# Attention sums of a graph layer: taken out of PSUM by ScalarE and added by GpSimd instead of VectorE

## What is computed

```python
deg = clip(adj.sum(axis=1), 1.0); dis = deg ** (-0.5)
diffusion = (dis[:, None] * adj * dis[None, :]) @ x - x
sim = x @ x.T / (norms[:, None] * norms[None, :])
attn = softmax(beta * sim * adj, axis=1)
x = layernorm(x + diffusion + sigmoid(alpha) * (attn @ x - x))
x = layernorm(x + relu(adj @ (x @ weights)))
```

## Time and profile before

| | before |
|---|---|
| median of 3 runs | 679.48 us |
| profiled execution: its time, its span | 679.01 us, 677.2 us |
| TensorE (PE) busy, share of the span | 652.0 us, 96% |
| VectorE (DVE) busy | 561.9 us, 83% |
| ScalarE (ACT) busy | 436.2 us, 64% |
| GpSimd (POOL) busy | 245.5 us, 36% |
| mean granted TensorE clock | 0.996 |
| DVE instructions L724 and L727 | 32 each, about 0.34 us each |

### The profile page before, as it was taken

The page is one execution under the profiler, slowest core; times in us unless marked ns, Lnnn a source line. Parts: engine busy times, 40 slices in busy tenths (PEclk is TensorE's granted clock), DMA queues, the critical chain, the costliest instruction groups (busy, mean ns, idle before and its releaser), DMA issues.

```text
span 677.2 us, 17913 instructions
## 1 busy us (share of the span) xinstructions
PE 652.0 (96%) x5623; PEld 517.4 (76%) x5623; DVE 561.9 (83%) x1678; ACT 436.2 (64%) x885; POOL 245.5 (36%) x229
## 2 busy tenths in 40 slices
PE   6679999999999999999999999899999999999997
PEld 6347777777777777777777776799888888888886
DVE  4879999999999999999999999767767766666664
ACT  5989998998999999989999988512222223111111
POOL 2899446455455464454464557300000000000000
PEclk8999999999999999999999999999999999999999
DMA  6589999999999999999999994300000000000000
GB/s 252 187 222 237 256 264 239 256 255 237 263 257 248 250 255 251 247 266 248 254 247 256 261 234 81 67 1 1 0 0 0 0 0 1 17 15 31 15 15 31
DMA packets 154538, 105.30 MB, mean 155 GB/s; under 512 B 135696, under 2 KB 136208, under 8 KB 154512
## 3 DMA queue, kind: packets, MB, share of 16 engines
q1 hardware_dynamic: 154080, 104.94, 61.1%
q10 hardware_dynamic: 432, 0.07, 0.1%
HBM read 69.34 MB, written 2.10 MB: 105 GB/s over the span
## 4 chain that ended last, share of the span: by engine, by line
PE 85%; DVE 5%; DMA 3%; POOL 3%; ACT 2%; SPq 1%; issue 1%; ACTq 0%; DVEq 0%; POOLq 0%
PE ps_e L1111 31%; PE ps_s L981 21%; PE ps_e L1013 8%; PE ps_e L992 7%; PE ps_acc L1013 7%; PE ps_e L1016 4%; PE ps_acc L1016 3%; DMA eTx<-e_parts 2%; DVE e_parts L717 2%; DMA col<-in_L_gnn_beta 1%; PE ps_e L1030 1%; DVE scores L696 1%; PE ps_at L965 1%; POOL x_parts L341 1%; PE ps_s L1030 1%
## 5 line engine op out<-in xcount | busy, mean ns | idle before, releaser
L981 PE MATMUL ps_s<-xn_parts,xn_signed 128*128 128x512 f16 x756 | 203.7, 379 | 5.5 <-DVE cmax L696 5.5
L696 DVE CUSTOM_DVE_ANT_1 scores<-ps_s,adj_bytes 128x512 f32<-128x512 f32 x252 | 171.4, 682 | 16.9 <-PE ps_s L981 9.3
L502 ACT ACTIVATE scores<-scores,col 128x1024 f32<-128x1024 f32 x128 | 157.4, 1232 | 4.5 <-DVE col L707 4.3
L326 POOL TENSOR_SCALAR e_parts<-scores 128x1024 f16<-128x1024 f32 x64 | 80.4, 1256 | 157.3 <-ACT scores L502 84.7
L448 ACT ACTIVATE adj_bytes<-land 128x1024 uint8<-128x1024 f32 x128 | 133.5, 1047 | 1.6 <-POOL packed L318 1.6
L1111 PE MATMUL ps_e<-x_parts,stage 128*128 128x256 f16 x1024 | 113.0, 273 | 0.0
L1111 PEld LDWEIGHTS ps_e<-x_parts,stage 128*128 128x128 fp8e4 x1024 | 100.2, 98 | 11.5
L1111 PE MATMUL ps_e<-y_parts,stage 128*128 128x256 f16 x896 | 105.4, 273 | 0.2
L981 PEld LDWEIGHTS ps_s<-xn_parts,xn_signed 128*128 128x128 f16 x756 | 69.5, 98 | 41.7 <-DVE cmax L696 5.5
L717 DVE SCALAR_TENSOR_TENSOR e_parts<-scores,e_parts 128x1024 f16<-128x1024 f32 x64 | 97.5, 1524 | 0.5 <-POOL e_parts L326 0.4
L509 ACT ACTIVATE eT_parts<-ps_e 128x512 f16<-128x512 f32 x128 | 75.7, 591 | 32.0 <-PE ps_e L992 31.4
(11 more groups left out here) (132 smaller groups left out, 992.2 us busy)
## 6 DMA issues: line engine op xcount, KB each, us to landing
land<-in_adj SPq DMA_DIRECT2D x128, 512.0 KB, 4.7
x_keep<-in_x SPq DMA_DIRECT2D x4, 512.0 KB, 8.6
out<-u SPq DMA_DIRECT2D x7, 256.0 KB, 2.0
eTx<-e_parts SPq DMA_TRANSPOSE x64, 5.1
out<-u SPq DMA_DIRECT2D x1, 192.0 KB, 1.9
eT_parts<-in_L_gnn_weights ACTq DMA_DIRECT2D x1, 64.0 KB, 8.7
scores<-in_L_gnn_weights SPq DMA_DIRECT2D x1, 64.0 KB, 2.5
out<-u SPq DMA_DIRECT2D x1, 64.0 KB, 1.6
```

Source lines behind the costliest of these rows:

```text
L326: nc.gpsimd.tensor_scalar(e_parts[:, n, 0, :], scores[:, q, (n + 2) * CH:(n + 3) * CH], E_SCALE, 1.0, ALU.mult, ALU.mult).wait_op(sign_don ...
L502: nc.scalar.activation(piece, piece, ACT.Exp, bias=neg_max[q], scale=abs_beta, accum_out=csum[:, q, i:i + 1]).then_inc(exp_done, 1)
L696: nc.vector.tensor_tensor_reduce(scores[:, q, o:o + BANK].rearrange("p (k q) -> p k q", k=K), score_bank(h, r == 0 if start else False).re ...
L981: ins = nc.tensor.matmul(score_bank(h, start), xn_signed[:, q, part, :], xn_parts[:, other, o:o + BANK], start=(part == 0 and other == 0), ...
```

## The change

For the row blocks 0 to 28 VectorE's `attn_add` is removed from its row program. In its place ScalarE gets `attn_out(r - 1, ...)` at the head of step 4 of row block r, ahead of `e_high`: one activation (copy with the per-partition scale `gain`) of the 256 columns from PSUM to a new SBUF tile `attn_sb` (128 x 256, f32, one buffer). It waits for the attends of that block (`attn_part`), for the adds of the block before that (`attn_added`, not in row block 1) and for the gain (`total_done`), and it signals `attn_read`. GpSimd gets `attn_add(r)`: two additions of 128 x 128, first half and second half of `attn_sb` onto `u`, the second behind the first by a semaphore. In its loop they stand after the two `ex_high` of block r+2 and ahead of the next `sign_block`; those of blocks 27 and 28 stand after `ex_high(R - 3, 1, 1)` and after `pack(R - 2, 0)`, the latter ahead of the degree instructions. Blocks 29, 30 and 31 stay on VectorE as they were, with the wait on `u_half` counted from there, and a wait for GpSimd's adds before the last one.

```diff
--- before.py
+++ after.py
@@ -93,6 +93,7 @@
         eTx = sb("eTx", [P, 2, 2, 2 * TC, P], F16)
         ident = sb("ident", [P, P], F32)
         col = sb("col", [P, 30], F32)
+        attn_sb = sb("attn_sb", [P, 2 * D], F32)
         packed = sb("packed", [P, 2, CH // K], U32)
         norm = sb("norm", [P, R], F32)
         norm_r = sb("norm_r", [P, R], F32)
@@ -173,6 +174,8 @@
         attn_part = sem("attn_part")
         u_half = sem("u_half")
         attn_read = sem("attn_read")
+        attn_half = sem("attn_half")
+        attn_added = sem("attn_added")
         total_done = sem("total_done")
         deg_step = sem("deg_step")
         deg_done = sem("deg_done")
@@ -341,6 +344,15 @@
                 nc.gpsimd.tensor_tensor(x_parts[:, q * TC:(q + 1) * TC, D:2 * D], u[:, q * TC:(q + 1) * TC, :],
                                         x_parts[:, q * TC:(q + 1) * TC, 0:D], ALU.subtract).then_inc(x_lo, 1)
 
+            def attn_add(r):
+
+                pool.wait_ge(attn_read, r + 1)
+                nc.gpsimd.tensor_tensor(u[:, bass.ds(r, 1), :], u[:, bass.ds(r, 1), :], attn_sb[:, 0:D].unsqueeze(1),
+                                        ALU.add).wait_op(sign_done, 1, "sem-ge").then_inc(attn_half, 1)
+                pool.wait_ge(attn_half, r + 1)
+                nc.gpsimd.tensor_tensor(u[:, bass.ds(r, 1), :], u[:, bass.ds(r, 1), :], attn_sb[:, D:2 * D].unsqueeze(1),
+                                        ALU.add).wait_op(sign_done, 1, "sem-ge").then_inc(attn_added, 1)
+
             def minus_x(q):
 
                 pool.wait_ge(x_lo, C)
@@ -375,21 +387,27 @@
             pack(2, 0)
             ex_high(2, 0, 0)
             ex_high(2, 0, 1)
+            pool.wait_ge(u_init, C)
+            attn_add(0)
             with pool.Fori(2, R - 5, 2) as r:
                 sign_block(r + 2, 0)
                 pack(r + 1, 1)
                 ex_high(r + 1, 1, 0)
                 ex_high(r + 1, 1, 1)
+                attn_add(r - 1)
                 sign_block(r + 3, 1)
                 pack(r + 2, 0)
                 ex_high(r + 2, 0, 0)
                 ex_high(r + 2, 0, 1)
+                attn_add(r)
             sign_block(R - 2, 0)
             pack(R - 3, 1)
             ex_high(R - 3, 1, 0)
             ex_high(R - 3, 1, 1)
+            attn_add(R - 5)
             sign_block(R - 1, 1)
             pack(R - 2, 0)
+            attn_add(R - 4)
 
             pool.wait_ge(cast_done, C * R)
             pool.wait_ge(deg_step, C)
@@ -509,9 +527,20 @@
                 nc.scalar.activation(eT_parts[:, b, 0, :], ps_e[:, b % 2, :], ACT.Copy,
                                      scale=E_SCALE).then_inc(e_hi, 1)
 
-            def row(r, q, start=False):
+            def attn_out(r, q, first=False):
+
+                act.wait_ge(attn_part, r * H + H)
+                if not first:
+                    act.wait_ge(attn_added, r)
+                act.wait_ge(total_done, 3 * r + 3)
+                nc.scalar.activation(attn_sb[:, :], attn_ps[q][:, 0:2 * D], ACT.Copy,
+                                     scale=gain).then_inc(attn_read, 1)
+
+            def row(r, q, start=False, second=False):
 
                 for h in range(H):
+                    if h == 4 and not start:
+                        attn_out(r - 1, 1 - q, second)
                     if h % 2 == 0:
                         e_high(r, h // 2, start)
                     if h < C:
@@ -526,7 +555,7 @@
             exps(0, 0, 1)
             cast(1, 1, 3, first=True)
             row(0, 0, start=True)
-            row(1, 1)
+            row(1, 1, second=True)
             with act.Fori(2, R - 3, 2) as r:
                 row(r, 0)
                 row(r + 1, 1)
@@ -723,7 +752,7 @@
                 dve.wait_ge(total_done, 3 * r + 3)
                 nc.vector.scalar_tensor_tensor(u[:, r, :], attn_ps[q][:, 0:D], gain, u[:, r, :],
                                                ALU.mult, ALU.add).then_inc(u_half, 1)
-                dve.wait_ge(u_half, r + 1)
+                dve.wait_ge(u_half, r + 4 - R)
                 nc.vector.scalar_tensor_tensor(u[:, r, :], attn_ps[q][:, D:2 * D], gain, u[:, r, :],
                                                ALU.mult, ALU.add).then_inc(attn_read, 1)
 
@@ -780,7 +809,7 @@
                 nc.vector.tensor_tensor(y_parts[:, q * TC:(q + 1) * TC, 1, :], x_keep[:, q * TC:(q + 1) * TC, :],
                                         y_parts[:, q * TC:(q + 1) * TC, 0, :], ALU.subtract).then_inc(y_lo, 1)
 
-            def row(r, q, start=False, second=False, spread=None):
+            def row(r, q, start=False, spread=None):
                 for h in range(H):
                     if h < C:
                         mask(r + 1, 1 - q, h + C, start)
@@ -794,10 +823,6 @@
                         row_max(r + 1, 1 - q)
                     if h == 3 and spread:
                         stage_block(spread[0], spread[0], (spread[1],))
-                    if h == 5 and not start:
-                        if second:
-                            dve.wait_ge(u_init, C)
-                        attn_add(r - 1, 1 - q)
                     if h == 6:
                         store_adj(r)
                     if h == 7:
@@ -806,7 +831,7 @@
                         total_step(r, q, (3, 4, 6).index(h), start)
 
             row(0, 0, start=True)
-            row(1, 1, second=True)
+            row(1, 1)
             with dve.Fori(2, R - 15, 2) as r:
                 row(r, 0)
                 row(r + 1, 1)
@@ -846,6 +871,7 @@
             for n in range(3):
                 total_step(R - 1, 1, n)
             stage_block(3, 3)
+            dve.wait_ge(attn_added, R - 3)
             attn_add(R - 1, 1)
             dve.wait_ge(dis_done, 2)
             dve.wait_ge(adj_stored, R)
```

## The result

The changed kernel takes 680.53 us, median of 12 runs from 679.35 to 683.00, against 679.51 us, median of 12 runs of the kernel before (678.94 to 680.87). The ratio is 1.0020, with a 95% interval of 1.0012 to 1.0027: 1.0 us slower, clear of the scatter of the runs, though less than the 0.3% that the prediction took as the least that can be told. A second group of runs, 11 of the same kernel, gave 680.50 against 679.08, 1.4 us more, and the ratio 1.0021 (1.0012 to 1.0030).

What follows compares the result with a forecast made beforehand. TensorE's own instructions bound the attention, 12.49 us per row block. To the profiled 679.01 us, +0.9 for late row blocks less 0.2 gave 679.7; the median lies 0.5 higher, so 680.2 us, range 678.3 to 683.8.

Steps and rivals of the forecast that it cites:

- TensorE sets the pace: In the attention TensorE is busy 50.00 of 50.00 us, 12.49 us per row block; the other engines have slack.
- ScalarE's instruction costs 0.45 us and nothing on the path: ScalarE's new PSUM read in each row block takes 0.45 us, hidden in idle time before a copy: cost 0.
- Rival C: ScalarE becomes late: third exponential 0.2 us later, 1.3 us over 26 row blocks, 680.8; chance 0.15.
- The adds push the first pack under the second subtraction, in half of the row blocks: GpSimd's adds shift its first pack against VectorE's second long subtraction, ending it 0.16 us later in 13 row blocks.
- the signs of being wrong: TensorE waits for masks, exponentials or DMA, 100-388 us; second subtractions over 1.5; ScalarE without idle time; square root after 414.
- rival A: The port decides: GpSimd makes VectorE's second subtraction 0.6 late, 685.3 to 691; chance of over 2.0 us slower 0.15.
- The cost lands as waits for the third exponential and for the DMA: Late row blocks exceed TensorE's margins of 0.16 (exponential) and 0.18 (DMA): 0.07 us on average in 13, +0.9 us.
- In the other row blocks nothing is lost: Where the first subtraction precedes GpSimd's copy, the adds are over before the second: no loss; growing margin, less 0.2 us.
- VectorE's saving is worth 0: Removing VectorE's pair from row blocks 0 to 28 frees 21 us of work that becomes idle time: 0 us.
- The end of the attention costs 0: From 388 to 442 us GpSimd's adds delay the degree chain 1.2 to 1.6 us, hidden: 0, with 0.4 either way.
- the 414 named as a sign of being wrong: At the attention's end, ScalarE's square root coming later than 414 us would show the prediction wrong.
- Rival B: VectorE was the hidden bound: 2.5 us gained from TensorE's end idle time and weight-load waits, 677.0; chance 0.06.

Runs made afterwards that it cites:

- e2: The changed kernel without GpSimd's two adds per row block and the waits on them (those sums missing from the result): 678.82 us, ratio 0.9996 to before.
- e4: The kernel before plus ScalarE's new 128x256 PSUM read into a spare tile, VectorE keeping its pair: 678.91 us, ratio 0.9998.
- e1: The changed kernel with GpSimd's two adds moved behind the packs, ahead of the first copy: 678.85 us, ratio 0.9996 to before.
- e9: The kernel before plus two spare GpSimd additions placed behind the packs, VectorE keeping its pair: 679.44 us, ratio 1.0004.
- e5: The changed kernel run again unedited, as a control: 680.50 us, ratio 1.0021 to before.
- e3: The kernel before plus two spare GpSimd additions in the place of the change's adds, VectorE keeping its pair: 681.95 us, ratio 1.0044.
- e6: The changed kernel with only one of GpSimd's two adds per row block (low half of those sums missing): 681.68 us, ratio 1.0041 to before.

## Why the prediction was right, and where it was not

The forecast was 680.2 us, and 0.7 us over before; measured are 680.53 and 1.0.

- *TensorE sets the pace.* Right. VectorE's relief without the adds gives 0.9996 (`e2`), and 288 us of attention hold only a few waits of TensorE.
- *ScalarE's instruction costs 0.45 us and nothing on the path.* Right: 0.46, ratio 0.9998 alone (`e4`). The copy behind it starts 0.03 us after its end (232.24 + 0.46, copy 232.73), and ScalarE goes on to wait for VectorE. Rival C falls with that.
- *The adds push the first pack under the second subtraction, in half of the row blocks.* Right in kind: 14 of 26 row blocks, +0.23 us (1.31 to 1.54) where +0.16 stood. The adds were mis-sized a little: 0.46 instead of 0.40, and 0.15 between the two instead of 0.08, and the first one, held back, took 1.31 where 0.85 to 1.2 was expected. Second subtractions of over 1.5 and waits for the exponential stood among the signs of being wrong; both came, in the small size. That is rival A's mechanism in the small size of the forecast. Moving the adds (`e1`) and leaving them out (`e2`) both take the whole cost away.
- *The cost lands as waits for the third exponential and for the DMA.* Shown for the first: 1.9 us (7 times) and 1.3 us (5 times) in two traces of the changed kernel, whose 24 row blocks are 2.0 and 1.2 us longer, against 0 to 0.4 us in `e1`, `e2`, `e4`, `e9` and the kernel before. The waits for the DMA (2.5 us against 1.4) rose in the profiled execution, but `e5` lists none and `e2`, which costs nothing, has 2.4, so I do not call them part of the cost. The forecast put 0.07 us on each of 13 row blocks; the traces have 0.27 on each of 7 and 5. That the sums nearly agree, 0.9 against 1.9 and 1.3, is in part luck.
- *In the other row blocks nothing is lost.* They even gained, 0.22 us per second subtraction, but not for the reason given: the prediction has the adds over before it, and they are not. Behind a kept-out copy the second add stands where a pack of 0.73 stood, and being shorter it is over sooner (after the change, GpSimd, then VectorE):

```profile
204.08 0.46 POOL L353 TENSOR_TENSOR u<-u,attn_sb 128x128 f32 x1 [0.16 <-POOL u L350]
```

```profile
204.22 1.40 DVE L746 SCALAR_TENSOR_TENSOR e_parts<-scores,e_parts 128x1024 f16<-128x1024 f32 x1
```

- *VectorE's saving is worth 0.* Right, in every pair of kernels that differ by it and at most by ScalarE's read besides: without the adds (`e2` against `e4`: 678.82 and 678.91), with them moved (`e1` against `e9`, ratios 0.9996 and 1.0004), and with them in the change's place as far as the traces show (24 row blocks of 301.7 and 300.9 us without the pair, 301.0 with it in `e3`). The medians alone would say otherwise, 2.8 us over before for `e3` and 1.0 for the changed kernel, but the excess lies behind the row blocks, where `e3` waits for its own semaphore. A run of `e3` without that wait was not made.
- *The end of the attention costs 0.* Right: 288.9 us from the last turn of the adjacency to the end, as before. The degree chain ended near 411.3 and its square root began at 416.9 behind a table load. That is later than the 414 named as a sign of being wrong, but the sign was badly set: before the change the root already began at 414.29, in a trace whose row blocks ended 2.6 us earlier. But the same table that I read there said where VectorE's relief would be worth something: in row block 29, which the change left on VectorE. Rival B had the right place and the wrong row blocks.

## What to carry to other kernels

Taking work off a nearly full engine gains nothing where another engine is full at 50.00 of 50.00 us; look for the stretch where the bound engine waits for it, here the last three of 32 row blocks, and move the work there alone: taking one pair of instructions off VectorE there, with the gain behind it put later, was worth 1.7 us, and 29 pairs elsewhere nothing. Before work goes to GpSimd, lay its timeline beside VectorE's instructions with two SBUF inputs and put it where none of them runs; the same two adds cost 1.0 to 1.4 us in one place of the row block and nothing in another. With contention of that kind less work can cost more (one add 2.6 us, two adds 1.4 in the same group), so a price per instruction is not enough: work out what is running when the critical instruction comes, in more than one row block. And where a median has no obvious cause, ask the trace in which stretch the time is lost: an experiment can bring a wait of its own, as `e3` did.

## What was unexpected in the hardware's behaviour

A VectorE subtraction of 128x1024 with both inputs in SBUF took 1.22 us where GpSimd ran nothing. Where a GpSimd instruction was running when it came, it ended 1.06 to 1.10 us after that instruction, in 45 to 49 of the 60 subtractions behind 60 us in each of five traces (before, after, `e3`, `e6`, `e9`): 1.53 us long behind a pack that ended at 230.58, 2.04 behind a copy that ended at 227.32, 2.91 behind a multiplication that ended at 426.77. GpSimd's add took 0.46 alone and 1.31 behind a subtraction. The lengths fit one waiting for the end of the other, whatever it is. VectorE's masks, with one input in PSUM, never changed length beside GpSimd (0.66 to 0.69 us in all traces), nor did its pair (0.34 to 0.35 before the change). A semaphore between two GpSimd instructions cost 0.15 us of idle time against 0.08 between instructions that do not wait.
